# Handing part of batch 0's rotation to POOL, reordering the first score units and moving the value projection in a one-core attention and expert kernel

## The reference

```python
ys = cond / sqrt(128)                                   # per batch, per feature
d = rsqrt((ys * ys) @ (weight * weight) + 1e-8)
xc = ((x * ys[:, None, :]) @ weight) * d[:, None, :]
q, k, v = split(xc @ w_qkv.T)                           # 16 heads of 8
q, k = rope(q), rope(k)
attn = softmax(causal(q @ k.T / sqrt(8)))
x = x + (attn @ v) @ w_out.T
x = x + zones(experts(x, cond))                         # shared and routed experts, then top-3 zones
```

## Time and profile before

| | us |
|---|---|
| median of 3 runs | 181.81 |
| the runs | 181.81, 184.06, 181.80 |
| span of the profiled execution | 180.1 |
| PE busy, whole span | 169.0 (94%) |
| DVE / ACT / POOL busy | 139.3 / 134.4 / 93.4 |

### The profile page before, as it was taken

The page is one execution under the profiler, slowest core; times in us unless marked ns, Lnnn a source line. Parts: engine busy times, 40 slices in busy tenths (PEclk is TensorE's granted clock), DMA queues, the critical chain, the costliest instruction groups (busy, mean ns, idle before and its releaser), DMA issues.

```text
span 180.1 us, 3258 instructions
## 1 busy us (share of the span) xinstructions
PE 169.0 (94%) x934; PEld 116.8 (65%) x934; DVE 139.3 (77%) x444; ACT 134.4 (75%) x224; POOL 93.4 (52%) x116
## 2 busy tenths in 40 slices
PE   6998989999999999988999999996999989999992
PEld 2765555765666666654648767874677867788881
DVE  5598899789898989981586998699889648637551
ACT  3569366687787788889735696953969999999970
POOL 4508188975453969696541632021769931676000
PEclk9999999999999999999999999999999999999999
DMA  4824673776666756421110799970760000001001
GB/s 132 305 46 103 179 208 118 231 257 233 177 203 187 198 181 184 157 78 49 58 55 9 217 294 361 338 229 11 234 233 0 0 4 0 0 2 58 0 4 58
DMA packets 15349, 24.28 MB, mean 135 GB/s; under 512 B 2844, under 2 KB 4828, under 8 KB 15308
## 3 DMA queue, kind: packets, MB, share of 16 engines
q1 hardware_dynamic: 14532, 23.29, 42.0%
q10 hardware_dynamic: 800, 0.79, 1.7%
HBM read 18.71 MB, written 5.27 MB: 133 GB/s over the span
## 4 chain that ended last, share of the span: by engine, by line
PE 70%; DVE 14%; ACT 8%; issue 5%; POOL 1%; ACTq 0%; DVEq 0%; POOLq 0%
PE psum L1405 11%; PE psum L1538 10%; PE psum L1466 9%; PE psum L1539 9%; PE psum L1540 9%; PE psum L1441 7%; DVE psum L772 4%; PE psum L1341 2%; PE psum L1355 2%; PE psum L1287 2%; ACT t_probs L1105 2%; PE psum L1445 2%; DVE t_raw L924 1%; PE psum L1400 1%; ACT t_q_pad L1155 1%
## 5 line engine op out<-in xcount | busy, mean ns | idle before, releaser
L772 DVE CUSTOM_DVE_ANT_0 psum<-psum,t_causal 128x128 f32<-128x128 f32 (+3 forms) x128 | 58.8, 525 | 6.0 <-PE psum L1405 3.3
L1105 ACT ACTIVATE t_probs<-psum 128x1024 f32<-128x1024 f32 (+2 forms) x48 | 40.8, 883 | 8.4 <-PE psum L1441 5.5
L1405 PE MATMUL psum<-t_stacked,t_q_pad 96*128 96x256 f32 (+2 forms) x104 | 32.1, 378 | 2.4 <-DVE t_row_max L772 1.2
L1405 PEld LDWEIGHTS psum<-t_stacked,t_q_pad 96*128 96x128 f32 x104 | 17.7, 188 | 16.3 <-DVE t_row_max L772 11.2
L672 POOL TENSOR_SCALAR_AFFINE_SELECT t_probs<-t_probs 128x512 f32<-128x512 f32 x32 | 20.5, 653 | 9.0 <-ACT t_probs L1105 8.3
L944 DVE SCALAR_TENSOR_TENSOR t_q_pad<-psum,t_zw_all,t_q_pad 128x512 fp32r<-128x512 f32 x24 | 17.8, 748 | 9.4 <-ACT t_q_pad L1153 9.3
L1139 ACT ACTIVATE psum<-psum 128x512 f32<-128x512 f32 x40 | 23.4, 586 | 1.2 <-PE psum L1540 0.6
L703 POOL TENSOR_TENSOR t_q_pad<-t_raw,t_q_pad 128x512 fp32r<-128x512 f32 x8 | 10.8, 1358 | 21.0 <-ACT t_q_pad L1155 21.0
L1466 PE MATMUL psum<-t_probs,t_v_all 128*32 128x512 f32 (+3 forms) x256 | 20.6, 439 | 0.0
L772 DVE DVE_READ_ACCUMULATOR2_ANT t_row_max<- 128x1 f32 x128 | 18.2, 142 | 0.0
L1153 ACT ACTIVATE t_q_pad<-psum,t_zw_all 128x512 fp32r<-128x512 f32 x24 | 16.5, 689 | 1.2 <-PE psum L1540 0.5
(11 more groups left out here) (232 smaller groups left out, 366.2 us busy)
## 6 DMA issues: line engine op xcount, KB each, us to landing
t_stacked<-scratch SPq DMA_DIRECT2D x16, 256.0 KB, 5.7
t_probs<-in_L_ffn_Wa SPq DMA_DIRECT2D x2, 1024.0 KB, 13.1
scratch<-t_o_sb SPq DMA_DIRECT2D x7, 256.0 KB, 2.0
t_raw<-in_experts SPq DMA_DIRECT2D x7, 256.0 KB, 3.1
t_stacked<-scratch SPq DMA_DIRECT2D x9, 192.0 KB, 2.7
t_q_pad<-scratch SPq DMA_DIRECT2D x28, 48.0 KB
scratch<-t_dn_hi SPq DMA_DIRECT2D x2, 512.0 KB, 3.2
t_q_two<-scratch SPq DMA_DIRECT2D x5, 192.0 KB, 2.6
```

What stands on the lines that cost most here:

```text
L772: last = V.tensor_tensor_reduce(scores, scores, causal[:, S - width:S], 1.0, 3 * BIG, ALU.add, ALU.max, row_max[s][:, qb, j:j + 1])
L1105: A.activation(o, scores, ACT.Exp, scale=float(1.0 / np.sqrt(np.float32(HD)))).then_inc(exp_done, 1)
L1405: last = T.matmul(bank[:, o:o + width], q_pad[s][0:TOP, j, qb * P:(qb + 1) * P], stacked[0:TOP, n, 0:width], start=True, stop=True)
```

## The change

It does six things, all in the first 36 us of the program.

1. For the second half of batch 0's tokens POOL, not DVE, does the addition and the low part, for q and for k.
2. `scores_for_max(0, 0..3)` stand ahead of the stacking of the second half, and ahead of `project(0)`. `project(0)` follows unit 5, `project_v(0)` unit 7, `project(1)` unit 9.
3. Five warm-up matmuls in place of eight, on a tile `warm` of their own. Six later ones: one behind the modulation of batch 0, one before each of units 1 to 3 (in the unit's own bank), and two before the stacking of the second half (bank 3).
4. V leaves the ring: both `project_v` write bank 6, the bank of the output product. `project_v(1)` moves out of the loop to a place behind `lay_max_under_q(0)`, `copy_v(1)` from behind `copy_qm(1)` to behind `exp(0, 2)`.
5. On ACT the scaling of batch 1 and `copy_q0(0)` come elsewhere, `copy_projection(0)` now stands ahead of `copy_q0(1)`, and the two DMAs of `spill(act, ...)` stand behind `copy_projection(1)`.
6. On SP the four DMAs of `pad_k(0)` stand together behind `load_k(1)`.

```diff
-WARM = 8
+WARM = 5
 @block.sync
             spill(sp, 1, 2, 1, spilled_1)
-            sp.wait_ge(pads_zero, 1)
-            pad_k(0, (0,))
             sp.wait_ge(spilled_1[0], 16 * SPILLS)
             sp.wait_ge(q1_zero, 1)
             pad_q(1)
             sp.wait_ge(spilled_1[1], 16 * SPILLS)
             load_k(1)
-            pad_k(0, (1,))
+            sp.wait_ge(pads_zero, 1)
+            pad_k(0)
 @block.gpsimd
-            pool.wait_ge(lo_ready, 4)
+            second = slice(S2, S)
+            for i in range(2):
+                pool.wait_ge(rope_ready, 3 + i)
+                G.tensor_tensor(roped[:, i, second], rope_t[i][1][:, 0, :], rope_t[i][1][:, 1, :],
+                                ALU.add).then_inc(roped_ready, 1)
+            for i in range(2):
+                pool.wait_ge(hi_ready, 3 + i)
+                G.tensor_tensor(qk_lo[:, i, second], roped[:, i, second], f32_of(qk_hi[:, i, second]),
+                                ALU.subtract).then_inc(lo_ready, 1)
 @block.vector
-            for h in range(2):
-                if h:
-                    dve.wait_ge(ld_rotb, 16)
-                rotate(0, h)
-                rotate(1, h)
-                add_turned(0, h)
-                add_turned(1, h)
-                take_low(0, h)
-                take_low(1, h)
+            for i in range(2):
+                rotate(i, 0)
+                add_turned(i)
+            take_low(0)
+            take_low(1)
+            dve.wait_ge(ld_rotb, 16)
+            rotate(0, 1)
+            rotate(1, 1)
 @block.scalar
-            modulated(1, xc[:, 1, :], psum[:, 2, :])
             place_q0(0, 0)
             copy_k0(0)
+            place_q0(1, 0)
+            place_q0(2, 0)
             take_hi_half(0, 1)
-            place_q0(1, 0)
+            place_q0(3, 0)
             take_hi_half(1, 1)
-            place_q0(2, 0)
-            place_q0(3, 0)
+            modulated(1, xc[:, 1, :], psum[:, 2, :])
+            copy_q0(0)
+            place_q0(0, 1)
             copy_k0(1)
-            for j in range(HG):
+            for j in range(1, HG):
                 place_q0(j, 1)
...
             copy_projection(0)
-            copy_q0(0)
             copy_q0(1)
             copy_v(0)
+            copy_projection(1)
             spill(act, 2, NG, 1, spilled)
-            copy_projection(1)
...
                 exp(n, 2)
+                if n == 0:
+                    copy_v(1)
 @block.tensor
             modulate_half(1)
+            keep_warm(1)
...
-            project(0)
-            scores_for_max(0, 0)
+            for u in range(HG):
+                scores_for_max(0, u)
+            keep_warm(2, psum[:, 3, :])
             stack_half(0, 1)
             stack_half(1, 1)
-            for u in range(1, len(MX_UNITS[0])):
+            for u in range(HG, len(MX_UNITS[0])):
                 scores_for_max(0, u)
-                if u == 6:
+                if u == 5:
+                    project(0)
+                if u == 7:
                     project_v(0)
-            project(1)
+                if u == 9:
+                    project(1)
             scores_for_max(1, 0)
             scores_for_max(1, 1)
             lay_max_under_q(0)
+            project_v(1)
             for u in range(2, FIRST):
...
-                if n == 0:
-                    project_v(1)
                 maximum(8)
```

More of the change, by code:

```diff
@@ L57 @@
 SPILLS = 2
-SLICES, LAY_AT = 11, 8
+SLICES = 11
 ST_ORDER = [("project", 0), ("project", 1)]
@@ L72, in max_units @@
     return MX_LIST[first + (end - first) * i // SLICES:first + (end - first) * (i + 1) // SLICES]
-RING_ORDER = [("max", 0, _u) for _u in range(7)] + [("v", 0)] + [("max", 0, _u) for _u in range(7, len(MX_UNITS[0]))]
+RING_ORDER = [("max", 0, _u) for _u in range(len(MX_UNITS[0]))]
 RING_ORDER += [("max", 1, _u) for _u in range(2)] + [("lay", 0)] + [("max", 1, _u) for _u in range(2, FIRST)]
 for _n in range(GROUPS):
-    RING_ORDER += [("max", *_u) for _i in range(LAY_AT) for _u in max_units(_n, _i)]
-    RING_ORDER += [("v", 1)] if _n == 0 else []
-    RING_ORDER += [("max", *_u) for _i in range(LAY_AT, SLICES) for _u in max_units(_n, _i)]
+    RING_ORDER += [("max", *_u) for _i in range(SLICES) for _u in max_units(_n, _i)]
 RING_ORDER += [("out", 0), ("route", 0)]
@@ L181, in program @@
         ident_r = sb("ident_r", [P, P], F32R)
+        warm = sb("warm", [P, BANK], BF16)
         minus_ident_b = sb("minus_ident_b", [P, P], BF16)
@@ L593, in _ @@
             G = nc.gpsimd
-            G.memset(max_pad[0][:], 0.0).then_inc(pads_early, 1)
+            G.memset(warm[:], 0.0).then_inc(pads_early, 1)
             G.memset(f32_of(sel[:, 0, :, :]), 0.0).then_inc(sel_zero, 1)
@@ L597, in _ @@
             G.memset(causal[:, 0:S - P], 0.0).then_inc(causal_zero, 1)
+            G.memset(max_pad[0][:], 0.0).then_inc(pads_early, 1)
             pool.wait_ge(ld_cond, 32)
@@ L1078, in copy_v @@
                     A.copy(v_cols[:, b * NG:(b + 1) * NG, kb, :, 0:HD],
-                           ring("v", b)[:, kb * P:(kb + 1) * P].rearrange("p (g j d) -> p g j d", g=NG, j=HG)
+                           PV[:, kb * P:(kb + 1) * P].rearrange("p (g j d) -> p g j d", g=NG, j=HG)
                            ).then_inc(v_copied, 1)
@@ L1282, in _, with keep_warm @@
             pe.wait_ge(pads_early, 1)
-            warm = max_pad[0][:].rearrange("p a b -> p (a b)")
-            def keep_warm(times):
+            def keep_warm(times, bank=psum[:, 0, :]):
                 for _ in range(times):
-                    T.matmul(psum[:, 0, :], warm[:, 0:P], warm, start=True, stop=True)
+                    T.matmul(bank, warm[:, 0:P], warm[:], start=True, stop=True)
             keep_warm(WARM)
@@ L1360, in project_v @@
                     pe.wait_ge(xc_ready[0], 1)
+                    pe.wait_ge(q0_placed, HG)
+                    pe.wait_ge(rep_copied, 2)
+                else:
+                    pe.wait_ge(v_copied, KB)
                 pe.wait_ge(xc_ready[1 + b], 1)
                 pe.wait_ge(ld_wv, 16)
-                wait_ring("v", b)
                 for kb in range(KB):
-                    last = T.matmul(ring("v", b)[:, kb * P:(kb + 1) * P], xc[:, b, kb * P:(kb + 1) * P],
+                    last = T.matmul(PV[:, kb * P:(kb + 1) * P], xc[:, b, kb * P:(kb + 1) * P],
                                     w_v, start=True, stop=True)
@@ L1395, in scores_for_max @@
                 bank = ring("max", n, u)
+                if n == 0 and 0 < u < HG:
+                    keep_warm(1, bank)
                 if len(pieces) == HG:
```

29 lines of the change are left out of this document (12 added, 17 removed).

## The result

| | before | after |
|---|---|---|
| median (us) | 181.97 | 185.80 |
| lowest and highest of 6 runs | 181.80, 184.06 | 184.30, 186.56 |
| the profiled execution | 181.81 | 184.30 |
| its span | 180.1 | 182.5 |

The changed kernel takes 1.0171 times as long, 95% interval 1.0119 to 1.0223. The forecast was 181.4 with a range up to 183.2: the time lies outside it, on the side of "slower". Where some runs of a kernel lie more than 1.5% above its lowest, the ratios here leave those runs out.

The account below looks back on a forecast made before the run. PE was taken as full from 36 us on, so only its 4.4 us idle before that could be won. 0.8 later by DVE and DMA and 1.2 less for V made 181.8 - 0.4 = 181.4 us, range up to 183.2.

Parts of the forecast that it names:

- the one on the spill: ACT's spill of k, issued at 21.6 instead of 19.1, lands at 25.3 to 26.1 and delays `load_k(2)`.
- a term of +0.8: Group 2's first unit starts later, waiting for `pad_q(2)` and DVE together: +0.8 us, bounds 0.3 and 1.5.
- the DMAs are the bound: Rival, 15%: spill lands late, queue loses another microsecond, group 2's first unit starts at 31.4; 182.4 us.
- V out of the ring: `project_v(1)` and its copy leave PE's chain at 32.21 to 34.02: -1.2 us, bounds 0.9 and 1.8.
- The start: With five warm-up matmuls the projections start at 6.5 instead of 6.91, 0.4 us earlier, bounds 0 and 0.8.
- The rival with 18%: A 0.8 us pause in the warm-up makes the clock rise late, so projections start at 1.2 GHz: 183.1 us.
- POOL's operation 0.70: Each addition or low part of the second half, with 256 elements, takes 0.70 us on POOL.
- DVE's idle time of 1.2 and 1.0 ahead of units 6 and 10: In units 4 to 11 DVE waits for PE, which has 5.9 us of work in one piece.
- unit 0, unit 4, unit 11 and the first maxima: On DVE the units start at 12.7, 16.2 and 22.5; the maxima are ready at 23.7, 0.75 later than before.
- What left DVE: Two additions and two low parts leave DVE's list for POOL: 1.4 us in all.
- the -0.4 of the sum: Whole kernel: 0.8 later by DVE and DMA, 1.2 less behind, so -0.4 us.

Follow-up runs that it names:

- spill_late_alone: The kernel before with only ACT's two spill DMAs moved behind `copy_projection(1)`: 186.58 us, ratio 1.0194.
- warm_in_wait: The changed kernel with eight matmuls on zeros in PE's list ahead of the wait for group 2's padded q: 184.47 us, ratio 1.0113.
- spill_back: The changed kernel with ACT's two spill DMAs ahead of `copy_projection(1)` again: 182.45 us, ratio 1.0007.
- before_v_out: The kernel before with only V's move out of the ring to the output product's bank: 182.45 us, ratio 0.9998.
- before_warm5: The kernel before with five warm-up matmuls in place of eight and nothing else: 184.41 us, ratio, from two runs, 0.9957.
- back_no_fill: The changed kernel with the spill ahead of `copy_projection(1)` again and without the six later matmuls on zeros: 185.27 us, ratio, from five runs, 0.9969.

## Why the prediction was wrong

- **The step that failed** is the one on the spill: "With up to 3.7 us to land it is there at 25.3 to 26.1". It landed at 27.95. The issue itself was forecast at 21.6 and came at 21.3 and 22.0. The landing was read from the lowest, median and highest of five transfers of the high part, 2.0, 2.9 and 3.7, of 128 to 512 KB and in their old places. The low part of k itself (128 KB) took 3.7 in its old place; here it took 5.95, in `spill_late_alone` 4.99 and in `warm_in_wait` 5.14 (issued at 22.25, `load_k(2)` at 27.41). "The transfers that ran beside the old spill are done by then", I wrote against the rival, but SP's own spills and `load_q(1)` ran beside the new one, and the DMAs were full until 26.0. `pad_q(2)` went out at 28.38, not 26.8, and the first unit at 31.52, not 30.3 to 30.5. The mechanism stood in the prediction twice, as a term of +0.8 and as the rival "the DMAs are the bound", whose first unit at 31.4 is what came. 1.93 is above the term's upper bound of 1.5.
- **What the rival's price left out** is the clock behind the wait: 1.18 by the books. I had thought of the clock only in the warm-up. A rival that puts PE at rest for 1.8 us should have carried this price. With the clock's 1.18, with 0.69 for V instead of 1.2, and with the first unit at 31.52 instead of 31.4, the rival's 182.4 becomes 184.2, and the profiled execution took 184.30.
- **V out of the ring**: -1.2 (bounds 0.9 and 1.8) was too much; measured 0.69 in `spill_back` and 0.68 in `before_v_out`. In both, PE then waits 0.52 for POOL's placement of the maxima; that this wait is the whole of the missing 0.5 is argued, not shown.
- **The start** was forecast at 6.5 and came at 5.90 in the profiled execution; the clock had risen in time. That is 1.0 earlier than before and outside my bounds of 0 to 0.8: x was there sooner than the 4.3 I took for it, since the first product on it starts at 4.05. In others the clock rises as late as 10.0, at up to 1.8 us on the projections (5.48 - 3.72). The rival with 18% was thus real, but not the cause: the runs of `spill_back` have it too (its median lies 1.1 above its lowest), and stay within 0.5 of the kernel before.
- **Right**: POOL's operation 0.70 (0.72 and 0.73), DVE's idle time of 1.2 and 1.0 ahead of units 6 and 10 (1.11 and 0.79), unit 0, unit 4, unit 11 and the first maxima in their order and spacing, each 0.4 to 0.5 earlier than forecast, behind a start that was 0.6 earlier. What left DVE was four operations of 0.42, not the 1.4 in all that I had; it changed nothing behind it. With the spill in its old place the profiled span is 179.8 against 180.1, -0.3, close to the -0.4 of the sum. But that is luck: two errors cancel there, the lateness of the first unit is 0.34 (DVE alone, since the spill's part is gone) and V gives 0.69, where I had 0.8 and 1.2.
- **The rule of the Trainium skill** that I weighed ("TensorE: Matmul & The Clock Gate", Part 1: the slow level is the default, activity releases it) fits the runs. `before_warm5` and `back_no_fill` agree with it: fewer matmuls on zeros, and seven and nine of twelve executions with a mean clock of 0.991 or less, against a third in the kernel before and none in `spill_back`. I had applied it to the start alone, and the loss came from PE's idle time at 29.6 to 31.5.

**Left open.** What held the last packets of the spill until 27.95, when the DMAs were nearly idle from 26.2. The timing speaks for an instruction fetch. In the list of DMA queues for 25 to 28 us (packets, MB, share of 16 engines' time) it is

```profile
q8 instruction: 1, 0.02, 2.4%
```

which is one packet of 1.16 us on one engine, from 25.66 to 26.82. ACT's queue is q10. Between 26.6 and 26.8 us no packet of any queue starts, and from 26.8 to 27.6 the last five of the spill do:

```profile
DMA packets 0, 0.00 MB, mean 0 GB/s; under 512 B 0, under 2 KB 0, under 8 KB 0
...
q10 hardware_dynamic: 5, 0.01, 5.5%
```

The first of the five starts at 26.81, as the fetch ends. In `spill_late_alone` the fetch takes from 26.22 to 27.50, no packet starts from 26.5 to 27.45, and the last four of the spill start from 27.49 on. In `warm_in_wait` it takes from 26.46 to 27.47, and there it is `load_q(1)` of SP's queue that goes on at 27.46, while the spill was through before. Three traces of three fit; but a packet doesn't tell its engine, and no run moved the fetch, so this is argued and not shown. An estimate of its part: 14 of the 16 shares of the transfer were complete by 25.98, the last at 27.48, 0.47 before the landing was told; without that tail of 1.5 us the landing would be at 26.45, and group 2's first unit at 30.0. `warm_in_wait` warns against making the tail the whole cause, for its spill took 5.14 us in full DMAs without it.

The median of the changed kernel lies 1.5 above its profiled execution. Its runs at 186.09 to 186.56 have mean clocks of 0.987 to 0.991, where the profiled one has 0.991; whether the landing or the clock makes up the rest there, no profile shows. One of the six, at 184.61, has a mean clock of 1.00: it lost about as much without the fall of the clock. A late first rise, which that mean doesn't count, could be what it lost instead. Nor does a profile show where the kernel before loses 2.2 us in a third of its runs.

## What to carry to other kernels

A DMA that a queue waits for is part of the path: when an instruction list is reordered, follow each DMA in it to who waits for its landing, and count what else is on the DMA engines at the new time, for a landing time read in the old place doesn't hold in the new one (3.7 us at most there, 5.0 to 6.0 here). Price a new wait of TensorE twice, once for its length and once for the clock behind it (here 1.9 and 1.2). A warm-up that looks too long buys agreement between executions, so compare medians of a dozen runs, not the best profile.

## What the runs showed of the hardware that I had not expected

- A transfer of 128 KB from SBUF to DRAM took 5.95 us: the DMAs were full for the first 4.0 of them and nearly idle for the last 1.7. The same transfer took 3.7 when it was issued 2.15 us earlier.
- In three traces a packet of 16 KB of instructions took 1.0 to 1.3 us, and the last packets of one transfer began within 0.02 us of its end, with no other packet starting for 0.2, 1.1 and 0.3 us ahead of that.
- An idle time of 1.87 us on PE was followed by a granted clock of 0.50 from 32.6 to 36.0. The clock fell 1.07 us after PE had resumed, not in the gap; in `spill_late_alone`, with a wait of 2.75, it fell within the wait. In `before_v_out` a wait of 0.76 was followed by 0.50 at once, from 18.4 to 21.8. Eight matmuls on zeros in the gap kept it up.
- In the profiled executions with five warm-ups the clock rose at 5.3, 5.5, 5.7, 6.5, 8.0, 9.0, 9.6 and 10.0 us, though PE's list up to the projections is the same in these eight kernels, but for one filler that two of them lack. In the six with eight warm-ups it rose between 4.7 and 7.0. In two of the late ones (8.0 and 9.0) PE also waited for the load of x, 0.36 and 0.22 us.
- Six matmuls on zeros that lie in PE's waits moved the share of executions with a mean clock under 0.995 from nine of twelve to none of twelve (`back_no_fill` against `spill_back`, which ran on another chip).
